# Layer 0's attention: the opening cut into pieces of one, one and two batches, and batch 7's division and output products regrouped

## The reference

```python
x = x + _L0_xattn_ref(_layernorm(x, axis=-1), ctx_4096, ctx_4096, ...)
x = x + _L0_ffn_ref(_layernorm(x, axis=-1), ...)       # 16 experts, top 4, and a shared expert
x = x + _L1_xattn_ref(_layernorm(x, axis=-1), ctx_4096, ...)
x = x + _L1_ffn_ref(_layernorm(x, axis=-1), ...)
```

## Time and profile before

| | |
|---|---|
| median of 3 runs | 1235.54 us (1235.32 to 1237.14) |
| the profiled execution, own time | 1236.74 us |
| its span, first to last instruction | 1235.4 us |
| mean granted TensorE clock | 0.990 |
| TensorE busy | 1186.4 us (96%) |
| VectorE / ScalarE / GpSimd busy | 65% / 54% / 34% |

### The profile page before, as it was taken

The page is one execution under the profiler, slowest core; times in us unless marked ns, Lnnn a source line. Parts: engine busy times, 40 slices in busy tenths (PEclk is TensorE's granted clock), DMA queues, the critical chain, the costliest instruction groups (busy, mean ns, idle before and its releaser), DMA issues.

```text
span 1235.4 us, 16581 instructions
## 1 busy us (share of the span) xinstructions
PE 1186.4 (96%) x5948; PEld 915.9 (74%) x5948; DVE 805.8 (65%) x1511; ACT 671.7 (54%) x1562; POOL 419.9 (34%) x515
## 2 busy tenths in 40 slices
PE   8989989999999999899999999999999999999997
PEld 5546546667776777688888888877888888888765
DVE  4457767677766784756666567764565666667856
ACT  2245741577777883355555555643455556556621
POOL 3413434577776762022222232310122222323100
PEclk9999999999999999899999999999999999999998
DMA  8774412875788677221112122212211121210101
GB/s 293 176 176 128 160 67 102 307 198 104 154 210 246 154 143 193 68 59 60 60 46 67 43 66 63 61 51 59 70 59 44 46 66 60 66 63 27 59 1 68
DMA packets 72849, 127.93 MB, mean 104 GB/s; under 512 B 11640, under 2 KB 30968, under 8 KB 70072
## 3 DMA queue, kind: packets, MB, share of 16 engines
q1 hardware_dynamic: 53024, 73.90, 19.6%
q0 software_dynamic: 17296, 48.26, 15.6%
q10 hardware_dynamic: 2448, 4.72, 1.1%
HBM read 150.37 MB, written 26.48 MB: 143 GB/s over the span
## 4 chain that ended last, share of the span: by engine, by line
PE 79%; DVE 7%; DMA 5%; ACT 3%; issue 3%; POOL 1%; SPq 1%; ACTq 0%; POOLq 0%; DVEq 0%
PE bank L466 48%; PE bank L1200 10%; PE bank L1988 7%; PE bank L1964 4%; PE bank L678 2%; DMA moe<-ys,token_out 2%; PE bank L692 2%; PE bank L1260 1%; PE bank L2303 1%; PE bank L644 1%; PE bank L659 1%; PE bank L1221 1%; DMA x<-in_x 1%; DMA q0st<-m0T 1%; DMA q_rows<-q0T_lo 1%
## 5 line engine op out<-in xcount | busy, mean ns | idle before, releaser
L1956 POOL TENSOR_SCALAR p<-p,mx 128x256 f32<-128x256 f32 x256 | 163.2, 654 | 522.4 <-DVE mx L1950 522.4
L1167 DVE TENSOR_TENSOR wf_lo<-wf_raw,wf_hi 128x512 fp32r<-128x512 f32 x188 | 121.6, 689 | 35.7 <-ACT wf_hi L1161 33.4
L1942 ACT ACTIVATE p<-bank,mx 128x256 f32<-128x256 f32 x256 | 118.1, 486 | 10.7 <-DVE mx L1932 10.6
L466 PE MATMUL bank<-xnA_hi,w1q_hi 128*128 128x512 f32 x288 | 118.6, 412 | 3.7 <-DVE xnA_lo L460 3.2
L1161 ACT ACTIVATE wf_hi<-wf_raw 128x512 fp32r<-128x512 f32 x192 | 110.1, 626 | 11.7 <-DMA wf_raw<-in_wffn,weight_row 11.7
L466 PE MATMUL bank<-xnA_hi,w1q_lo 128*128 128x512 f32 x288 | 114.7, 398 | 0.0
L466 PE MATMUL bank<-xnA_lo,w1q_hi 128*128 128x512 f32 x288 | 114.1, 396 | 0.0
L1971 ACT ACTIVATE p1T_hi<-bank 128x512 fp32r<-128x512 f32 x128 | 75.2, 596 | 65.6 <-PE bank L1964 65.6
L1896 ACT ACTIVATE q1T_hi<-bank 128x512 fp32r<-128x512 f32 x64 | 38.3, 598 | 132.4 <-PE bank L466 132.4
L466 PE MATMUL bank<-w1o_hi,a1T_hi 128*128 128x512 f32 x256 | 105.2, 411 | 0.1
L1902 DVE TENSOR_TENSOR q1T_lo<-bank,q1T_hi 128x512 fp32r<-128x512 f32 x64 | 44.2, 691 | 93.3 <-ACT q1T_hi L1896 93.3
(11 more groups left out here) (338 smaller groups left out, 2963.7 us busy)
## 6 DMA issues: line engine op xcount, KB each, us to landing
w_raw<-in_wq SPq DMA_DIRECT2D x64, 256.0 KB, 2.6
w_raw<-in_wo SPq DMA_DIRECT2D x64, 256.0 KB, 2.7
moe<-xn SPq DMA_DIRECT2D x2, 2304.0 KB, 10.9
returned<-moe SPq DMA_DIRECT2D x8, 512.0 KB, 7.2
q0st<-q_rows SPq DMA_DIRECT2D x14, 256.0 KB, 4.5
x<-in_x SPq DMA_DIRECT2D x8, 256.0 KB, 5.3
ctx<-in_ctxT SPq DMA_DIRECT2D x2, 1024.0 KB, 10.2
q_rows<-q0T_hi ACTq DMA_DIRECT2D x8, 256.0 KB
```

Of the source, the lines that this page charges most:

```text
L466: ins = nc.tensor.matmul(ps, a, b, start=(n == 0), stop=(n == len(pairs) - 1))
L1167: nc.vector.tensor_tensor(wf[m % 2][1][:, a, c, :], raw[m % STREAMS][:, a, c, :], wf[m % 2][0][:, a, c, :].bitcast(F32), ALU.subtract).the ...
L1942: ins = nc.scalar.activation(pr1[s % 2][:, h, :], banks.of(("s1", s, n))[:, hh * 2 * P:(hh + 1) * 2 * P], ACT.Exp, bias=m[:, UH + h:UH + h ...
L1956: ins = nc.gpsimd.tensor_scalar(pr1[s % 2][:, h, :], pr1[s % 2][:, h, :], m[:, 3 * UH + h:3 * UH + h + 1], 1.0, ALU.mult, ALU.mult)
```

## The change

**The opening.** Half 0 is now projected in three pieces: batch 0, batch 1, and batches 2 and 3 together (`PIECES`); half 1 stays whole as piece 3. Each piece has its own keys, four query blocks, splits, stores and semaphore counts. Piece 0 waits for the norm of batch 0 alone; the norms of batches 1 to 3 follow. The high parts are stored by ScalarE, the low parts by SP. SP's list starts with batch 0, the key weight, batch 0's context and the query weight; the rest of `x` for half 1 and its context come after the loads of batch 0's queries. The last two blocks of piece 2, all values of half 0, the norm of half 1, the keys and queries of half 1 (in halves of two products), and the values of half 1 move into the unit loop. The output weight is loaded later and its high parts are taken at steps `j` = 19 to 22.

```diff
-        QUERY_AT = {KV0 + 2: 1, KV0 + 4: 2, LEAD_S + 5: 3}
-        QUERY_OUT_AT = {3: 0, KV0 + 3: 1, KV0 + 5: 2, LEAD_S + 6: 3}
+        QUERY_AT = {KV0 + 3: (3, 0), KV0 + 5: (3, 1), KV0 + 7: (3, 2), KV0 + 9: (3, 3), 1: (2, 2), 3: (2, 3)}
+        OUT_WEIGHT_AT = {2 * KV0 + 3 + k: k for k in range(KT)}
+        KEYS_AT = {KV0 + 1: 3}
+        STATS1_AT, SQRT1_AT, TURN1_AT = 0, 4, 5
+        PIECES = [(0, 0, P), (0, P, 2 * P), (0, 2 * P, HT), (1, 0, HT)]
-        VALUES_AT = {KV0 - 1: (HB, HB + 1), KV0: (HB + 2,), KV0 + 1: (HB + 3,)}
+        VALUES_AT = {**{HB + k: k for k in range(HB)}, **{3 * KV0 - 1 + k: HB + k for k in range(HB)}}
...
             # SP's list
+            for piece in range(2):
+                keys_lo_out(piece)
+                for m in range(KT):
+                    queries_lo_out(piece, m)
+                keys_in(piece)
+                queries_in(piece)
+                if piece == 0:
+                    for b in range(HB, B):
+                        load(x[:, b, :], A["x"][b]).then_inc(S["ld_x_rest"], 16)
+                    load(ctxT[1][:, :, :], A["ctxT"][1]).then_inc(S["ld_ctx01"], 16)
+            keys_lo_out(2)
             for m in range(KT):
+                queries_lo_out(2, m)
             keys_in(2)
             queries_in(2)
             queries_in(3)
+            maxima(0)
+            keys_lo_out(3)
+            queries_lo_out(3, 0)
+            load(bo[:, :], A["bo0"].broadcast_to([P, D])).then_inc(S["ld_wbo0"], 16)
+            load(wo_raw[:, :, :], A["wo0"]).then_inc(S["ld_wbo0"], 16)
...
             # TensorE's list
+            norm_turn(0, 0, 0)
+            keys(0, 7)
+            for m, n in enumerate((4, 5, 6, 0)):
+                query(0, m, n)
+            for k in range(1, HB):
                 norm_turn(0, k, k)
+            keys(1, 7)
+            for m, n in enumerate((4, 5, 6, 0)):
+                query(1, m, n)
+            keys(2, 1)
+            for m, n in enumerate((2, 3)):
+                query(2, m, n)
...
             # ScalarE's list
+            norm_sqrt(0, 0, 1)
+            norm_hi(0, 0)
+            norm_sqrt(0, 1, HB)
+            for piece in range(2):
+                keys(piece)
+                for m in range(KT):
+                    query(piece, m)
+                    if m == 0:
+                        keys_hi_out(piece)
+                    else:
+                        queries_hi_out(piece, m - 1)
+                queries_hi_out(piece, KT - 1)
+                if piece == 0:
+                    for k in range(1, HB):
+                        norm_hi(0, k)
```

```diff
-        GATE_AT, GATE_OUT_AT, PRELOAD_AT = UNITS0 + 2, UNITS0 + 4, UNITS0 + 10
+        GATE_AT, GATE_OUT_AT, PRELOAD_AT = UNITS0 + 4, UNITS0 + 10, UNITS0 + 10
+        LAST_PRODUCTS_AT, LAST_ADD_AT = UNITS0 + 5, UNITS0 + 9
...
-                if piece:
-                    if piece[0] == B - 1:
-                        tensor_gate_up(0, piece[1])
+                if piece and piece[0] < B - 1:
                     project_out(*piece)
+                if 0 <= i - LAST_PRODUCTS_AT < G0:
+                    if i == LAST_PRODUCTS_AT + 1:
+                        tensor_gate_up(0, 0)
+                    project_out(B - 1, i - LAST_PRODUCTS_AT)
+            tensor_gate_up(0, *range(1, KT))
...
+            divided(B - 1, 0)
+            for n in range(1, G0):
+                divided(B - 1, n)
+                remainder(B - 1, n - 1)
+            remainder(B - 1, G0 - 1)
             gpsimd_rank_consts(1)
-            attended(B - 1)
```

More of the change, by code:

```diff
@@ L531, in keys_in @@
                 sp.wait_ge(S["zeroed"], b % KRING + 1)
-                sp.wait_ge(S["st_k"], 32 * (half + 1))
+                stored, count = KEYS_STORED[piece_of(b)]
+                sp.wait_ge(S[stored], count)
                 if b >= KRING:
@@ L611, in tensor_attention0, with keys @@
         def tensor_attention0():
[L612 to L619 removed]
+            srs, trs = cycle((0, 1, 6)), cycle((2, 3))
+            def keys(piece, n, part=range(KT)):
+                half, first, last = PIECES[piece]
+                if part[0] == 0:
+                    banks.take(n, ("k0", piece), (S["k0_lo"], piece + 1))
+                    pe.wait_ge(S["ld_wk0"], 32)
+                    if piece:
+                        pe.wait_ge(S[f"ld_ctx0{half}"], 16)
+                ps = banks.of(("k0", piece))
+                for k in part:
+                    ins = nc.tensor.matmul(ps[:, first:last], wkv[:, 0, k, :], ctxT[half][:, k, first:last],
+                                           start=(k == 0), stop=(k == KT - 1))
+                if part[-1] == KT - 1:
+                    ins.then_inc(S["k0_mm"], 1)
             def values(b, n):
@@ L627, in values, with query @@
                                       for k in range(KT)]).then_inc(S["v0_mm"], 1)
-            def query(half, m, n):
-                ps = banks.take(n, ("q0", half, m), (S["q0_lo"], half * KT + m + 1))
-                pe.wait_ge(S["xn_ready"], HB * (half + 1))
-                pe.wait_ge(S["ld_wq0"], 16)
-                mm_group(ps[:, :], [(wq[:, k, m * P:(m + 1) * P], xnF[half][:, k, :])
-                                    for k in range(KT)]).then_inc(S["q0_mm"], 1)
+            def query(piece, m, n, part=range(KT)):
+                half, first, last = PIECES[piece]
+                if part[0] == 0:
+                    banks.take(n, ("q0", piece, m), (S["q0_lo"], piece * KT + m + 1))
+                    pe.wait_ge(S["xn_ready"], HB * (half + 1) if piece else 1)
+                    pe.wait_ge(S["ld_wq0"], 16)
+                ps = banks.of(("q0", piece, m))
+                for k in part:
+                    ins = nc.tensor.matmul(ps[:, first:last], wq[:, k, m * P:(m + 1) * P], xnF[half][:, k, first:last],
+                                           start=(k == 0), stop=(k == KT - 1))
+                if part[-1] == KT - 1:
+                    ins.then_inc(S["q0_mm"], 1)
             def scores(i):
```

323 lines of the change are left out of this document (166 added, 157 removed).

## The result

The changed kernel takes 1256.64 us (median of 4 runs, 1253.25 to 1257.9) where the kernel before takes 1235.43 (4 runs, 1234.98 to 1237.14) beside it: ratio 1.0158, interval 1.0140 to 1.0176. It is 21 us slower, and the prediction, 1232.2 with a range of 1228 to 1238.5, is wrong in sign. The profiled execution took 1257.08 us, its span 1255.8, granted clock 0.982 (before: 0.990).

A forecast was written before the change was run, and what follows sets the result against it. TensorE was taken as nearly full throughout layer 0's attention, leaving idle time and low-clock stretches to win. Terms 0.2 - 2.2 - 1.3 = -3.3 us took the profiled 1236.74 to 1233.4, the median to 1232.2; range 1228 to 1238.5.

The forecast's parts named there:

- step 4: Opening, unit 12: first turned scores wait for batch 0's maxima, queued in SP's list behind loads; landing at about 51.0.
- steps 1 to 3: Opening up to unit 12: norms, splits, projections by piece, eight units paced by VectorE; first scores 27.5 to 29.2, unit 12 at 48 to 49.5.
- Rival R4: Opening: small stores cost like large ones, maxima land near 57, S is 72; +2.5 to +3 us, 1238.3; chance 0.20.
- S: The time at which TensorE starts unit 19, predicted as 65.7.
- Step 5: Units 12 to 18: scores, turned scores and half query blocks, 13.1 us for units 12 to 17, bringing unit 19 to 65.7.
- Step 6: Unit 19 on: GpSimd's wo_lo and eight bias adds precede its first division; TensorE stands 5 us, first product at 84.7; +0.2 us.
- Term B: Unit 32: batch 4's keys are asked for earlier, so the stall of 2.2 us goes; -2.2 us.
- Term C: End, gate's first product to the next norm's turns: nothing waits after the change; -1.3 us, bounds -0.8 and -1.6.

The follow-up runs named there:

- e8: Changed kernel with batch 0's maxima ahead of the loads of batches 2 and 3, and the 2 MB issued before the first low-part store: ratio 1.0072.
- e1: Changed kernel with one move in SyncE's list, the DMA of batch 0's maxima ahead of the loads of batches 2 and 3: ratio 1.0060.
- e3: Changed kernel with batch 0's maxima ahead of the loads of batches 2 and 3, and the 2 MB issued by GpSimd: ratio 1.0050.
- e14: e3 with scratch high/low parts outside the heads, two banks for the last queries, and the output weights' 1 MB issued earlier by GpSimd: ratio 1.0007.
- e4: The kernel before with the change's end alone, the opening as before: -1.1 us, interval 0.9979 to 0.9999.
- e16: The kernel of e4 again, on another chip, beside e15: ratio 0.9985 against the kernel before, -2.1 us.
- e15: e14 with GpSimd's eight bias additions ahead of its four remainders of the output weights: ratio 1.0028.
- e12_loads_early: Changed kernel with maxima ahead, two banks, bias later, and 3 MB of loads before the first low-part store: first scores wait 7.79 us; total not given.

## Why the prediction was wrong

**Where it failed: step 4, the landing of batch 0's maxima: 51.0 predicted, 67.6 measured.** The step had the right transfer, the right place in SyncE's list and the right order; its times were wrong in three places, which make up the 16.6 us: 13.4 for the landing of piece 2's stores, 1.4 for the twelve issues and 1.8 for the landing of the maxima. It let piece 2's stores land at 38.9 (52.3), because it took the loads and stores of piece 1 as off the path: it never asked what piece 1's stores share the DMA engines with. The 2 MB of `x` and context are issued right in front of them, as the diff shows, and the last of them takes 9.71 us to land, where it takes 4.4 in e8 with nothing so large in front. All that SyncE does is one series of issue and landing, so this shifts piece 2, then batches 2 and 3. And it gave the twelve load issues 6.3 us; they took 7.7; the maxima then took 7.5 us to land, where it had 5.7. What made this cost 12 us on TensorE is the maxima's place: ready at 49.6, issued at 60.06. e1 shows that part alone (-11.9 us). It also shows what step 4 could not have saved: with the maxima early the first turned scores come at 57.44 and not at 51.0. So 10.2 of the 16.6 us are SyncE's list, and 6.4 were lost before it, in steps 1 to 3.

**Rival R4** named this outcome (late pieces, maxima near 57, slower) and had its price and its size wrong. (Its working also has two slips: "less 3.5" should be the sum's 3.3, and the S at which the sum is zero 69.0.) Small stores do not cost like large ones, 1.5 us each: batch 0's four landed 4.7 us after the first issue, while ScalarE's four landed beside them. The bytes of others are what acts in piece 1. The Trainium skill's rule that stood beside R4, "DMA: Bandwidth & Descriptors", section Rules for kernel authors, is for transfers under 64 KB; these are of 64 KB, and no run here tests it by itself.

**Step 5, 14.7 us from the maxima to S, is off by 4.4** (19.1 measured; 18.7 in e1, at full clock throughout that stretch). Two terms are missing. One is the single bank for the last query blocks: the first half of one waits 1.09 us for VectorE's remainder of the one before, twice here and three times in e1. The other is the clock: the first 4 us behind the 9.19 us of idle run at a granted clock of 0.56, and the same rows take 1.8 us longer there than in e1.

```profile
75.31 1.98 PE L673 MATMUL bank<-xnF,wq 128*128 128x512 f32 x4 [1.09 <-DVE q0T_lo L947]
...
93.66 9.87 POOL L1050 TENSOR_TENSOR x<-x,bo 128x512 f32<-128x512 f32 x8
...
104.05 0.46 POOL L1070 TENSOR_TENSOR a<-num,den 128x128 f32<-128x128 f32 x1 [0.28 <-DVE den L971]
```

**Step 6, S to the first product, 19.0 predicted, 21.05 measured.** The run itself came as the step has it, `wo_lo` from S + 2.0 and the bias adds to S + 16.8, but it did not hold TensorE here. It ended at 103.5, the first division waited 0.28 us for VectorE and not for it, and the product's last operand was ready at 105.4, 2.4 us before TensorE came to it: 3.16 us at batch 3's keys and the 7 us at low clock behind them had taken its time. It does hold TensorE in e3 and e14 (3.2 and 3.55 us), where the maxima are early. The three errors, 16.6 + 4.4 + 2.05, are the 23.1 us between the predicted 84.7 and 107.80. That the last is small is luck: other idle time and a low clock stood where the step had its 5 us of idle.

**Term B, -2.2 predicted, -2.0 measured** (lateness of the exponentials: 23.3 us at the first product, 21.4 at unit 32's, and constant to unit 63). Term B's cause, the stall at unit 32, is gone as predicted, but 3.16 us of the same kind now stand at unit 24. **Term C, -1.3 predicted, -1.2 measured**, and shown alone by e4 and e16. **Steps 1 to 3** were 2 to 10 us early: the query weight landed at 11.5, the moments were complete at 14.7 (11.4), first scores came at 31.24 (27.5 to 29.2), the eighth unit's scores at 45.06 (its maximum at 40 to 41.7) and unit 12 at 57.64 (48 to 49.5). Between them stand waits that the steps do not have, 2.53 us for VectorE's norm of half 1 among them, and 6 us at a granted clock of 0.50 (41 to 47). In the changed kernel all of this lies in front of the wait of 9.19 us and costs nothing; in e1 it is the path.

**What is left of the opening.** Repaired in every way tried, it stands at 1.0007 (e14) where the end alone gives 0.9985 to 0.9989: some 2 us worse than the old opening, with intervals that overlap. On one chip, e15 at 1.0028 and e16 at 0.9985 have intervals well apart. TensorE's list up to the first product holds 435 matmuls where it held 356, and in e1 it stands idle 18.0 us in that stretch against 9.6 before. Each wait taken away was followed by another (maxima of batch 1, GpSimd, maxima of batch 3). Two waits stand in every run with the divided opening and were never taken away, here as the changed kernel has them:

```profile
21.07 3.81 PE L673 MATMUL bank<-xnF,wq 128*128 128x128 f32 x32 [1.77 <-ACT xnF L451]
...
41.34 1.09 PE L443 MATMUL bank<-consts,xn 128*128 128x128 f32 x4 [2.53 <-DVE xn L434]
```

The first is 1.3 to 3.1 us in the runs and the second 1.2 to 2.5. Whether the remainder is these two, or the sum of many landings in series, no run tells; either is argued from the traces.

The version to keep is that of e4_end_only: the old opening with the new end, faster than the kernel before by 1 to 2 us as far as two intervals that end at 0.9999 and 0.9997 can tell, and clearly faster than the changed kernel.

## What to carry to other kernels

Before costing a list that issues transfers, write down for each wait in it what was issued in front of it, on any queue, and how many bytes: here a store of 64 KB took as long as the megabytes it shared the engines with. A transfer that is ready early belongs ahead of loads that are needed later, even in a list that seems to have time. And cutting a stage in pieces turns one landing into several in series: count landings as well as bytes, and expect each removed wait to show the next.

## What the runs showed of the hardware

Batch 0's last low-part store, 64 KB, landed in 2.5 us in the changed kernel, in 5.2 with 2 MB of loads issued ahead of it (e8_rest_early) and in 10.3 with 3 MB (e12_loads_early). Piece 1's landed in 9.7 us with 2 MB just in front and in 4.4 without; moving the 2 MB to another issuing engine left it at 10.7. A DRAM-side pattern of 8 by 16 rows moved at 220 GB/s in a window where 128 rows moved at 354. A granted clock of 0.51 for 7 us followed 3.16 us of idle of TensorE. And the profiled openings of one and the same kernel differ: the last exponential came at 161.97 in e4_end_only and 157.02 in e16_end_only, so a single trace places a difference in the opening only beyond some 5 us.
